# A tile moved by 32 rows: two on-chip transfers from ScalarE's queue in place of a second TensorE transpose

## The reference

```python
x = x + 0.5 * _L0_ffn_ref(_layernorm(x), ...)
x = x + _L0_attn_ref(_layernorm(x), ...)
x = x + 0.5 * _L0_ffn_ref(_layernorm(x), ...)
```

```python
for i in range(DEPTH):
    x = attn_layer(shift_tokens(x), Wqkv[i], q_scale[i], k_scale[i], Wo[i]) + x
    x = ffn_layer(shift_tokens(x), ln_g[i], ln_b[i], W1[i], b1[i], W2[i], b2[i]) + x
```

## Time and profile before

| | us |
|---|---|
| median of 3 runs | 3437.93 |
| lowest, highest | 3436.97, 3445.19 |
| the profiled execution | 3436.08 |
| its span | 3434.3 |

### The profile page before, as it was taken

One profiled execution on the slowest core, in us unless ns is written; L12 is line 12 of the kernel. 1 busy time (PEld: TensorE's weight loads), 2 busy tenths in 40 slices (PEclk: granted clock), 3 DMA queues, 4 the chain that ended last, 5 costly groups with the idle time before them and its releaser, 6 DMA issues. The chain is left out here.

```text
span 3434.3 us, 102986 instructions
## 1 busy us (share of the span) xinstructions
PE 3243.5 (94%) x42016; PEld 2206.8 (64%) x42016; DVE 2964.2 (86%) x5370; ACT 2531.7 (74%) x4368; POOL 2536.8 (74%) x1357
## 2 busy tenths in 40 slices
PE   6999999999999999996997899999999999999997
PEld 3666666666666666664554566666666666666664
DVE  6989999899999899983577899899999999899994
ACT  4778777877778777872575687778777878787873
POOL 6878888888888888860002888888888888788881
PEclk8999999999999999997798999999999999999998
DMA  2110010010010000002000000000000000000000
GB/s 80 49 31 2 21 31 2 20 31 2 21 31 2 21 18 2 2 2 78 1 2 1 2 2 2 33 2 2 33 2 2 33 2 2 33 2 2 2 2 13
DMA packets 31050, 53.30 MB, mean 16 GB/s; under 512 B 11510, under 2 KB 24054, under 8 KB 27254
## 3 DMA queue, kind: packets, MB, share of 16 engines
q1 hardware_dynamic: 30582, 46.71, 4.1%
HBM read 37.26 MB, written 9.44 MB: 14 GB/s over the span
## 5 line engine op out<-in xcount | busy, mean ns | idle before, releaser
L428 POOL TENSOR_TENSOR arena<-arena 128x1024 f32<-128x1024 f32 x384 | 723.2, 1905 | 400.2 <-DVE arena L531 400.2
L421 POOL TENSOR_TENSOR arena<-arena 128x1024 f32<-128x1024 f32 x384 | 907.3, 2363 | 30.1
L412 POOL TENSOR_TENSOR arena<-arena 128x1024 f32<-128x1024 f32 x384 | 767.4, 1998 | 55.9 <-ACT arena L759 42.5
L998 PE MATMUL ps_a<-w_qk,stream 128*128 128x512 f32 x1536 | 759.2, 617 | 16.4 <-DVE arena L541 11.4
L1013 PE MATMUL ps_h<-arena,w_vo 128*128 128x256 f32 x3072 | 730.7, 381 | 5.8 <-issue 4.0
L759 ACT ACTIVATE arena<-ps_a 128x512 f32<-128x512 f32 x768 | 418.8, 601 | 317.2 <-PE ps_a L998 308.1
L1013 PEld LDWEIGHTS ps_h<-arena,w_vo 128*128 128x128 f32 x3072 | 563.4, 191 | 79.0 <-issue 7.7
L541 DVE TENSOR_TENSOR arena<-ps_a,arena 128x1024 f32<-128x1024 f32 x384 | 467.1, 1216 | 54.7 <-ACT arena L759 54.6
L547 DVE TENSOR_REDUCE arena<-arena 128x16 f32<-128x1024 f32 x384 | 462.9, 1205 | 37.0 <-ACT arena L765 37.0
L991 PE MATMUL ps_t<-ident,arena 128*128 128x128 f32 x3072 | 402.7, 274 | 27.5 <-ACT arena L770 20.5
L765 ACT ACTIVATE arena<-arena 128x1024 f32<-128x1024 f32 x384 | 413.5, 1077 | 8.7 <-ACT arena L759 0.4
(11 more groups left out here) (146 smaller groups left out, 5007.0 us busy)
## 6 DMA issues: line engine op xcount, KB each, us to landing
w_qk<-fWqkv SPq DMA_DIRECT2D x12, 1024.0 KB, 5.3
vo_scr<-w_vo SPq DMA_DIRECT2D x6, 1024.0 KB, 5.6
w_vo<-vo_scr SPq DMA_DIRECT2D x6, 1024.0 KB, 7.3
arena<-fWqkv SPq DMA_DIRECT2D x6, 512.0 KB, 8.0
arena<-fWo SPq DMA_DIRECT2D x6, 512.0 KB, 8.5
w<-fW SPq DMA_DIRECT2D x12, 192.0 KB, 6.2
w<-fW SPq DMA_DIRECT2D x6, 341.0 KB, 3.3
w_scr<-w SPq DMA_DIRECT2D x6, 341.0 KB, 7.3
```

Source lines behind the costliest of these rows:

```text
L412: pool.tensor_tensor(swapped.rearrange("p (c d) -> p c d", d=DH), raw[n].rearrange("p (c d) -> p c d", d=DH), tab.unsqueeze(1).to_broadcas ...
L421: pool.tensor_tensor(r, r, swapped, ALU.add).then_inc(add_s, 1)
L428: pool.tensor_tensor(r, r, rn[u % 2][:, n * HEADS:(n + 1) * HEADS].unsqueeze(2) .to_broadcast([P, HEADS, DH]), ALU.mult).then_inc(rot_s, 1)
L998: last = pe.matmul(A[:, n * 512:(n + 1) * 512], stream[:, c0:c0 + P], w_qk[:, u // TILES % 2, off:off + 512], start=True, stop=True)
```

## The change

PE makes one transpose a unit, for plane 1. ACT copies 128 columns and no longer 256. Then ACT waits for the end of its own copy and issues two transfers from on-chip memory to on-chip memory: rows 0 to 95 of plane 1 go to rows 32 to 127 of plane 0, and the last 32 rows of the previous unit's plane 1 go to rows 0 to 31. Each adds 16 to one of three semaphores `shifted`; the means of unit v wait for both transfers of v, and a copy that overwrites a plane waits for the transfers that read it. `shifts` counts how many units have used a semaphore. The three `x_win` buffers now lie inside the zeroed part of the arena, since the first unit reads the "previous" buffer.

```diff
+def shifts(block, u):
+    return block * (UNITS // 3) + u // 3 + 1 if u >= 0 else 0
...
         k_t = [carve(PAIRS * (WIN + P)).rearrange("p (c t) -> p c t", c=PAIRS) for _ in range(2)]
+        x_win = [carve(2 * D).rearrange("p (k d) -> p k d", k=2) for _ in range(3)]
         zeroed = used[0]
-        x_win = [carve(2 * D).rearrange("p (k d) -> p k d", k=2) for _ in range(3)]
...
+        shifted = [sem(f"shifted{n}") for n in range(3)]
...
                     act.wait_ge(xw_ps, st.tiles(u))
                     wait(act, mean_ps, st.tiles(u - 3))
-                    act.activation(x_win[u % 3].rearrange("p k d -> p (k d)"), S[:, 512:512 + 2 * D], ACT.Copy)\
-                       .then_inc(xw_sb, 1)
+                    here, before = x_win[u % 3], x_win[(u - 1) % 3]
+                    wait(act, shifted[(u + 1) % 3], 32 * shifts(st.block, u - 2))
+                    if u == 0:
+                        act.wait_ge(zero_done, st.block + 1)
+                    act.activation(here[:, 1, :], S[:, 512:512 + D], ACT.Copy).then_inc(xw_sb, 1)
+                    act.wait_ge(xw_sb, st.tiles(u))
+                    act.dma_start(here[WIN:P, 0, :], here[0:P - WIN, 1, :]).then_inc(shifted[u % 3], 16)
+                    act.dma_start(here[0:WIN, 0, :], before[P - WIN:P, 1, :]).then_inc(shifted[u % 3], 16)
...
                     c0 = PAD + u % TILES * P
-                    for k in range(2):
-                        last = pe.transpose(S[:, 512 + k * D:512 + (k + 1) * D],
-                                            stream[:, c0 - WIN + k * WIN:c0 - WIN + k * WIN + P], ident[:])
-                    last.then_inc(xw_ps, 1)
+                    pe.transpose(S[:, 512:512 + D], stream[:, c0:c0 + P], ident[:]).then_inc(xw_ps, 1)
...
                     pe.wait_ge(xw_sb, st.tiles(v))
+                    pe.wait_ge(shifted[v % 3], 32 * shifts(st.block, v))
```

## The result

| | before | changed |
|---|---|---|
| median of 16 runs, us | 3441.64 | 3452.38 |
| lowest, highest | 3431.27, 3452.04 | 3444.46, 3460.92 |
| ratio, 95% interval | | 1.0034 [1.0023, 1.0045] |
| the profiled execution, its span | 3436.08, 3434.3 | 3455.75, 3454.0 |

By the ratio the change makes the kernel slower by 0.34%, 11.7 us (the two medians lie 10.7 us apart), and the interval excludes 1. Forecast was 3434 against 3437.93, a little faster. The measured 3452.38 lies inside the stated range of 3426 to 3458, but the time moved the other way.

What follows compares the result with a forecast made beforehand. It took TensorE's chain, with waits on ScalarE and VectorE, to set each 30.62 us pair; -0.11 + 0.02 + 0.05 = -0.04 us, times 96 = -4 us, gave 3434 against 3437.93, range 3426 to 3458.

Steps and rivals of the forecast that it cites:

- the chain that sets the pair: Second FFN block: one transpose less saves 0.11 us in the even step, where it is on the path, 0 in odd.
- The place of the loss: Odd step: scores wait for the halo copy, which ends 0.97 us later against 0.99 cover; 0.05 us taken.
- two issues: ScalarE, between copy and halo copy: issuing both transfers takes 0.85 us with gaps, from SyncE's rows of these shapes.
- ScalarE's part: Shorter copy, lost overlap, wait for own result and issues: halo copy ends 0.97 us later, odd step loses 0.05.
- The wait for the copy's result: ScalarE, before the issues: waiting for its own copy to end adds 0.08 us.
- the dear case: Rival: issues dearer on ScalarE, halo copy holds the scores in odd steps; 3454 us with issues like 0.51, chance 0.34.
- The case of two issues of 1 us: Within the dearer-issues rival: 2.1 us for both, even steps lose 0.9, odd 1.2; +190, 3620 us.
- TensorE's added wait: Before the means, even step: the new wait for the transfers costs 0.02 us, bounds 0 and 0.055.
- Landing: The transfers' arrival before the means: hidden, with one pair of steps, 30.62 us, to hide in.
- The larger memset: GpSimd, before the block: 2560 to 3328 columns, 2.23 to 2.90 us, twice, ending before the first projection; cost 0.
- VectorE's room of 0.2 us: Even step: VectorE could start about 0.2 us sooner, so the 0.11 us transpose saving arrives whole.
- estimate of 3428: Whole kernel, if dispatch takes about 50 ns: both issues 0.1 us, halo copy with 0.7 us to spare in odd steps.

Runs made afterwards that it cites:

- e3: The changed kernel with one transpose and the short copy, but neither transfers nor their waits; pair 30.51 us, ratio 0.9927 to the kernel before.
- e5: The kernel before with only the three buffers put in the zeroed area and ScalarE waiting for the zeros; pair 30.62 us, ratio 0.9988.
- e1: The changed kernel with the wait and both transfers put behind the halo copy, ahead of the copies of the means; ratio 0.9933 to the kernel before.
- e6: The changed kernel with the two transfers issued by SyncE instead of ScalarE; pair 30.52 us, ratio 0.9900 to the kernel before.
- e7: The changed kernel with the wait and both issues put behind the copies of the means; pair 30.70 us, ratio 0.9957 to the kernel before.

## Why the prediction was wrong

**Right:** the chain that sets the pair. In the earlier trace rows L1123 was read as on the path in even steps and covered in odd ones; e3 measured 0.11 and 0.00 us. The place of the loss was right too: the halo copy, in odd steps, with a cover of 0.99 us. In the changed kernel the halo copy ends 2.12 us after the copy's start instead of 0.80, 1.32 us later, and 1.32 - 0.99 = 0.33 is what the scores lose. Most even steps lost nothing, though 0.3 us was said to be left and 0.015 was; where the second issue was a long one they lost too, 5.3 us in all, for which the prediction had nothing.

**Wrong, the step that failed:** the term "two issues" in ScalarE's part. The prediction had 0.33 + 0.045 + 0.43 + 0.045 = 0.85 us; measured were 0.53 + 0.03 + 0.62 + 0.10 = 1.28 us. The wait for the copy's result took 0.03 and not 0.08, so from the copy's end to the halo copy's start it is 1.31 us in place of 0.93. The 0.43 came from rows of the same shape, and the 0.33 from a row after a wait, but all of them read from or wrote to memory off the chip. I took the rows nearest in shape and called them the size, when the cover was spent to 0.02 us on this very number. SyncE's queue in the same trace had single issues of 0.52 and 0.58 us as well (L341 and L309, at 27.7 and 34.1 us), which the prediction doesn't weigh. The error of 0.38 us turned the forecast of -0.04 us a pair into +0.22 in the most frequent one, -4 us into +21, and with the second issue's tail into +30 over all steps.

**Luck in the dear case.** Two issues of 0.51 gave 3454, at a chance of 0.34, and 3452.4 came. The mechanism is that of this case. The closeness is luck: the loss by waits is larger than the case had (30 us net and not 16), and 8 to 12 us fewer holes, which nobody forecast, took part of it back. The base moved as well, from the 3437.93 of 3 runs to 3441.64. (The case of two issues of 1 us is mis-added there: 3437.9 + 190 is 3628, not 3620.)

**Smaller:** the copy is 0.107 us shorter in odd steps, where 0.10 was said. TensorE's added wait costs nothing: L1134 to the means went down by 0.109, all of the transpose; I had 0.02. Landing takes 1.9 us in the median, 8.2 at most, against a pair of steps. The larger memset can't be told from nothing (e5). VectorE's room of 0.2 us was enough.

**The rule on dispatch.** The traces show 0.52 to 0.62 us for an issue on either queue. The Trainium skill, DMA: Bandwidth & Descriptors, section "Anatomy of one DMA — SWDGE (gpsimd) path", lists about 50 ns for the sequencer's dispatch, on GpSimd's path. GpSimd issues no transfer in any of these kernels, so no run here tests that figure for its own path. The prediction's estimate of 3428, by that figure for ScalarE's queue, isn't met by this order of instructions. With the issues moved to where nothing waits (e1) the time goes below it, 0.9933 x 3437.9 = 3415, with their length unchanged, so the gain is one of place and not of a shorter dispatch.

**Not foreseen:** that the queue can issue while the engine works, so that the same 1.15 us is free a few lines further down. Ratio 0.9933 for e1 and 0.9900 for e6 show that the idea was worth having, in another place: both are faster than the kernel before and the changed one.

## What to carry to other kernels

A transfer's issue is an instruction of its own on the queue that makes it, here of 0.5 to 0.6 us and now and then over 1 us: before moving one there, list what is queued behind it and who waits for that, and put the issues where the next instruction waits anyway or a long one is running. Where the cover is equal to the cost within a tenth, the answer is not "about zero" but two cases of which the dearer needs its full weight, above all if no row shows that kind of transfer on that queue. A short work item that others wait for (the halo copy here) goes ahead of long ones that nobody needs for two steps. And add a loss up over all steps before you compare it with the measured time: the most frequent step leaves out the tails.

## What the runs showed of the hardware

- An issue of a transfer from on-chip to on-chip memory of 96 rows of 512 bytes takes 0.53 us on ScalarE's queue and 0.52 on SyncE's; one of 32 rows right behind it 0.62 and 0.60, at times up to 1.55 us. It lands 1.9 us after its issue.
- ScalarE's queue issues while an ACTIVATE ahead of it still runs, if the wait before the issue is met: in e1 from 2506.07 beside one that runs until 2506.43 us, in e7 from 2514.62 beside one that runs until 2515.30.
- The scores' 128 matmuls (1.485 us) take 1.575 us in e7, where two issues fall beside them; the 0.09 us is lost later where the issues come later.
- TensorE stands still for up to 3.8 us at a time (e7), with no wait in the trace, and 287 of the 288 such holes inside the scores' runs lie a multiple of 256 of its instructions apart. They open at 17 to 29 of the 173 to 181 such places there, 16 to 28 us of an execution, and in part at different ones from run to run.
